# Matmuls of tiles 0, 2 and 4 extended over 16, 32 and 56 columns of the next tile in a fused convolution kernel

## The reference

```python
def _L0_conv_ref(x, dw_weight, pw_weight, pw_bias):
    h = conv_general_dilated(x, dw_weight, padding=((1, 1), (1, 1)), feature_group_count=C)   # 3x3 depthwise
    h = gelu(h)
    maps = einsum('bchw,oc->bohw', h, pw_weight) + pw_bias[None, :, None, None]
    maps = maps.reshape(B, 8, C, H, W)
    out = zeros_like(x)
    for i, (dx, dy) in enumerate(OFFSETS8):
        diff = roll(x, shift=(dy, dx), axis=(-2, -1)) - x
        out = out + maps[:, i] * diff
    return out

x = x + _L0_conv_ref(_gn(x), dw_weight, pw_weight, pw_bias)
```

## Time and profile before

| | |
|---|---|
| runs shown | 2279.0 and 2280.24 us, median 2279.62 us |
| span of the profiled execution, first to last instruction | 2255.6 us |
| median less span | 24.0 us |
| TensorE matmul busy | 2201.9 us, 98% of the span, 10752 matmuls |
| VectorE busy | 2067.1 us, 92% |
| mean granted TensorE clock | 1.000 |

### The profile page before, as it was taken

How to read it: one execution, slowest core, us unless ns; L and a number is a source line. 1 busy time by engine, 2 the same in 40 slices (tenths; PEclk the granted TensorE clock), 3 DMA queues, 4 the chain that set the end, 5 groups by cost and what they waited for, 6 DMA issues and landing times.

```text
span 2255.6 us, 28700 instructions
## 1 busy us (share of the span) xinstructions
PE 2201.9 (98%) x10752; PEld 2014.8 (89%) x10752; DVE 2067.1 (92%) x2234; ACT 1842.6 (82%) x2762; POOL 1976.3 (88%) x857
## 2 busy tenths in 40 slices
PE   1999999999999999999999999999999999999998
PEld 1999999999999999999999999999999999999997
DVE  7999999999999999989999899999999999989895
ACT  5979888798888978888788887878878788787774
POOL 5889998999989988898888988889889998988985
PEclk9999999999999999999999999999999999999999
DMA  6245372543626444263443725337254372543424
GB/s 180 49 84 118 50 143 62 107 97 56 150 33 123 98 84 105 50 129 76 90 99 51 145 58 102 88 64 157 33 106 96 53 155 34 106 99 50 98 33 74
DMA packets 47083, 202.13 MB, mean 90 GB/s; under 512 B 3040, under 2 KB 7136, under 8 KB 45664
## 3 DMA queue, kind: packets, MB, share of 16 engines
q0 software_dynamic: 30192, 94.97, 26.1%
q1 hardware_dynamic: 16752, 105.34, 18.2%
HBM read 104.88 MB, written 146.80 MB: 112 GB/s over the span
## 4 chain that ended last, share of the span: by engine, by line
PE 92%; DVE 5%; ACT 1%; issue 1%; DMA 0%; POOL 0%; SPq 0%; DVEq 0%; ACTq 0%
PE psum L914 92%; DVE psum L775 2%; DVE products L702 1%; DVE psum L784 1%; DVE psum L702 0%; DMA acc<-x 0%; ACT psum L587 0%; ACT psum L555 0%; DVE acc L724 0%; ACT hid L569 0%; DVE acc L756 0%; POOL hlo L332 0%; DVE fields L807 0%; DVE part_sums L794 0%; DVE products L759 0%
## 5 line engine op out<-in xcount | busy, mean ns | idle before, releaser
L587 ACT ACTIVATE psum<-psum,bias,rstd 128x448 f32<-128x448 f32 x1792 | 1203.9, 694 | 368.6 <-PE psum L914 364.1
L914 PE MATMUL psum<-hhi,w_hi 128*128 128x448 f32 x3584 | 1312.7, 366 | 46.1 <-ACT hhi L574 45.4
L363 POOL TENSOR_TENSOR acc<-acc,products 128x896 f32<-128x896 f32 x333 | 1162.7, 3491 | 205.5 <-DVE products L702 197.6
L914 PE MATMUL psum<-hhi,w_lo 128*128 128x448 f32 x3584 | 1311.7, 366 | 0.0
L914 PE MATMUL psum<-hlo,w_hi 128*128 128x448 f32 x3584 | 1022.3, 366 | 0.3 <-POOL hlo L332 0.3
L784 DVE SCALAR_TENSOR_TENSOR psum<-xn,dw_f,psum 128x896 f32<-128x896 f32 x768 | 881.5, 1148 | 72.4 <-ACT psum L559 66.7
L914 PEld LDWEIGHTS psum<-hhi,w_hi 128*128 128x128 f32 x3584 | 671.9, 187 | 109.7 <-issue 45.4
L914 PEld LDWEIGHTS psum<-hlo,w_hi 128*128 128x128 f32 x3584 | 671.5, 187 | 62.2 <-POOL hlo L332 0.9
L914 PEld LDWEIGHTS psum<-hhi,w_lo 128*128 128x128 f32 x3584 | 672.0, 187 | 61.3
L702 DVE TENSOR_TENSOR products<-psum,fields 128x896 f32<-128x896 f32 x555 | 600.9, 1083 | 24.1 <-ACT psum L587 22.8
L702 DVE TENSOR_TENSOR acc<-psum,fields 128x896 f32<-128x896 f32 x224 | 241.6, 1086 | 45.8 <-ACT psum L587 45.3
(11 more groups left out here) (67 smaller groups left out, 448.2 us busy)
## 6 DMA issues: line engine op xcount, KB each, us to landing
out<-acc POOLq DMA_DIRECT2D x96, 896.0 KB, 7.7
out<-x SPq DMA_DIRECT2D x16, 3136.0 KB, 12.8
xpad<-x SPq DMA_DIRECT2D x30, 1568.0 KB, 14.8
out<-acc POOLq DMA_DIRECT2D x15, 448.0 KB, 5.6
acc<-x SPq DMA_DIRECT2D x4, 784.0 KB, 6.8
xpad<-pw_t SPq DMA_DIRECT2D x1, 2048.0 KB, 12.2
out<-products SPq DMA_DIRECT2D x2, 224.0 KB, 1.9
dw_f<-dw SPq DMA_DIRECT2D x1, 9.0 KB, 8.1
```

What stands on the lines that cost most here:

```text
L363: nc.gpsimd.tensor_tensor(a, a, p, ALU.add).then_inc(added_s, 1)
L587: nc.scalar.activation(m, m, ACT.Identity, bias=bias[ip][:, g, d:d + 1], scale=rstd[ip][:, g:g + 1]).then_inc(biased_s, 1)
L914: last = nc.tensor.matmul(maps(n0 * UNITS + q)[:, side, :], w[:, kk, col:col + P], h_part(h, t, nl, kk), start=s == 0, stop=s == len(steps ...
```

## The change

`make_maps` gets a width for each tile: 448 columns, and for tiles 0, 2 and 4 of every image 464, 480 and 504. The moving operand then runs on over the first 16, 32 or 56 columns of the odd tile behind it in the slot, and the output into columns 448 and up of the same bank, which nothing reads. Number and order of the instructions, weights, waits and signals stay.

```diff
+        def maps_wide(q, width):
+
+            b = 2 * (q % MAP_GROUPS)
+            return psum[:, b:b + 2, 0:width]
+
...
+        def h_wide(h, t, nl, kk, width):
+
+            if width == PX:
+                return h_part(h, t, nl, kk)
+            return h[:, H_SLOT[nl - t + 2 * (t // 2) + kk]].rearrange("p t x -> p (t x)")[:, 0:width]
...
         @block.tensor
         def _(pe):
+            SPILL = {0: 16, 2: 32, 4: W}
+
             def make_maps(n0, nl, u):
 
                 t, q = nl % TILES, nl * UNITS + u
 
+                width = PX + SPILL.get(t, 0)
...
-                        last = nc.tensor.matmul(maps(n0 * UNITS + q)[:, side, :], w[:, kk, col:col + P], h_part(h, t, nl, kk),
+                        last = nc.tensor.matmul(maps_wide(n0 * UNITS + q, width)[:, side, :], w[:, kk, col:col + P],
+                                                h_wide(h, t, nl, kk, width),
                                                 start=s == 0, stop=s == len(steps) - 1)
```

## The result

The changed kernel takes 2332.3 us (2330.95 and 2333.62), the kernel before 2279.6: slower by 52.7 us, where 27.9 were forecast. The quotient of these medians is 1.023; the ratio of the runs near the fastest of each kernel is 1.0247, 95% interval 1.021 to 1.0285. The profiled execution of the changed kernel took 2330.95 us with a span of 2329.2, so 1.8 us lie around the span, and not 24.0. The kernel before turns out to scatter by 3% from one execution to the next (2213 to 2280 us over 71 timed runs, these two among them), so the experiments are told by median and range, and the size of the slowdown depends on which of its executions one compares with: it is 2.3% against the two here, and 5% against the quickest. The 1.8 us already say that the profiled execution of before (span 2255.6) and its two timed runs (2279.6) weren't equally long.

The account below looks back on a forecast made before the run. The prediction took TensorE's stream of 10752 matmul steps to bound the kernel. Added columns +66.6, slow steps -46.6, redrawn pace +10.2 and stalls -2.3 gave +27.9 us on 2279.6, that is 2307.5 us, range 2250 to 2370.

Parts of the forecast that it names:

- The 24.0 us around the span: Whole run: 24.0 us of the 2279.6 us were taken to lie outside the profiled span of 2255.6 us.
- two-pace reading: TensorE's matmul stream in the profile: the same matmul steps at 200.0 or 206.7 ns, about 6980 of 10752 at the latter.
- The 46.6 us of slow steps: TensorE: 6980 matmuls at 206.7 ns cost 6.7 ns each over 200.0 ns; 46.6 us was subtracted.
- The pace is drawn anew some 96 times: Borders of tiles 0, 2 and 4: six step-length changes per image each redraw the pace, some 96 times instead of 7.
- one slow step in seven: All 10752 matmuls after the change: a seventh at 206.7 instead of 200.0 ns, adding 10.2 us; ends 0 and 71.7.
- rival A: From the border of tiles 0 and 1, first image, every matmul pays 20.0 ns over its stream: 2369 us; chance 0.30.
- The upper value: Wide tiles 0, 2, 4: each added column costs 0.4167 ns, steps of 206.7, 213.3 and 223.3 ns, 66.6 us in all.
- rival B: Wide tiles: columns nearly free, steps of 200.0 ns up to 480 columns and 210.0 at 504; 2255 us; chance 0.24.
- the 0.11 us between two weight loads: Stalled place at 130.74 us: next load starts at 130.85, so loads aren't what a step waits for and columns cost.
- The sign that the prediction named for a failure on columns: Wide tiles' steps not 6.7, 13.3 and 23.3 ns over their neighbours' would mean the column cost is wrong.
- The six waits: Unit 2 of tile 4: six stalls waiting for VectorE, 2.3 us in all, vanish because tile 4's first 24 matmuls take longer.
- Rival C: Whole stream: a disturbance brings steps to their bare stream length, 186.7 ns at 448 columns; 2152 us; chance 0.06.

Follow-up runs that it names:

- only0: Kernel before with tile 0 alone of each image widened, by 16 columns; 2284.2 us.
- after_again: The changed kernel run again without an edit; 2331.8 us median of 4 runs (2331.4 to 2334.8).
- narrow: Kernel before with tile 1 of image b cut to 448 - 8 b columns (448 to 328), leaving out columns of the result; 2199.4 us.
- ladder: Kernel before with tiles 0, 2 and 4 of image b at 448 + 4 b columns (448 to 508); 2307.1 us.
- mend: The changed kernel with the last unit (12 matmuls) of tile 0 at 500 columns instead of 464; 2297.3 us (2296.3 to 2298.1, 4 runs).

## Why the prediction was wrong

**The time around the span: wrong, 22 of the 24.0 us.** "The 24.0 us around the span" failed. Every later run has 1.7 to 1.9 us there. The profiled execution of before was quick for a third of its length; its two timed runs, at 2279.0 and 2280.2 us, lie where a stream slow from the start does (2255.6 + 25.1 - 2.3 + 1.8 = 2280.2). The text used the two-pace reading within the trace and didn't ask whether another execution would share it. The 46.6 us of slow steps, taken as something the change would give back, was 71.7 us in the runs that were the yardstick, and is 0 in others.

**The pace: wrong, and the step that mattered most.** "The pace is drawn anew some 96 times" failed, and with it the one slow step in seven. A change of width is no draw. Single wide matmuls left the quick pace in 24 of 32 cases, near the six of seven assumed, but in all 29 cases that can be compared the second execution did as the first. A wide tile of 96 equal matmuls settles into a repeating pattern, and what it hands on follows from its width and what it found: slow after slow at all 44 wide tiles behind the one that threw the changed kernel's profiled run, quick after quick behind 480 and 504 in its image 0. Of the change's widths only 464 turned quick to slow, at both tiles (one here, one in only0) that found the quick pace and ended at that width. Since no width of the change leads back and the stalls are gone, slow is the end of every run. What does vary from run to run is the start and the stalls, which the prediction counted with the borders as one kind of disturbance. The mechanism is rival A's, with its place right (the border of tile 0) and its image off by one, or not at all in after_again, which is slow from tile 1 of image 0 on. Its price of 2369 us was high by the misread 24.0 us (22 of it) and by the column costs below.

**The columns: right in kind, short in size on the quick pace, long on the slow one.** "The upper value", stream plus 13.3 ns, was named as a bound from above; over the quick step 464, 480 and 504 columns cost 12.2, 16.7 to 17.8 and 26.7 ns instead of 6.7, 13.3 and 23.3; over the slow step 5.5, 10.0 and 20.0. That they cost at all, against rival B, was argued from the 0.11 us between two weight loads, and narrow and ladder bear it out. The sign that the prediction named for a failure on columns came: the wide tiles' steps aren't 6.7, 13.3 and 23.3 ns over their neighbours'. The slope that the Trainium skill gives (TensorE: Matmul & The Clock Gate, "Back-to-back issue gap") is borne out on the mean: from 328 to 508 columns the step grows by 77.7 ns, where 180 / 2.4 is 75.0. Its 2.5 ns of fixed cost, which that section gives for an isolated matmul and not for a stream of weight loads and matmuls, fits no row here, the least being 12.3.

**The stalls: right for the profiled execution.** The six waits are gone, with the cover of tile 4's first 24 matmuls. A slow stream has no stall, so the timed runs of before, if slow throughout, had no 2.3 us to give back.

**The sum with what was measured.** From the profiled execution of before: columns over the quick step 1536 x (12.2 + 16.7 + 26.7) ns = +85.4; 60 slow tiles x 96 x 6.67 ns = +38.4, in place of the 46.6 before; stalls -2.3: +74.9, against 73.6 us between the spans. From the timed runs, slow throughout: 1536 x (5.5 + 10.0 + 20.0) ns = 54.5, less image 0's four quick tiles, 2.6: +51.9, against 52.7. Term by term against the forecast: columns 54.5 for 66.6, slow steps -2.6 for -46.6 + 10.2 = -36.4, stalls 0 for -2.3. The slow steps are thus 33.8 us off, more than the whole miss of 24.8, and the columns hid a part of it. That the two timed runs of before were slow throughout is inferred from their times; no trace of one is kept. Rival C's third pace was never seen at 448 columns.

## What to carry to other kernels

Where one engine's step repeats ten thousand times, read the distance of its starts along the whole span before anything else: two stable values are possible at one granted clock, and a single profile then doesn't stand for the timed runs. Check that the profiled execution's span plus a small constant gives the timed run; a gap of 1% is another execution, not overhead. Columns that cost little a piece can cost much by what they leave behind (34 us between the changed kernel and mend), and a short stretch of the right width can fix the pace; which width that is has to be measured. Before calling an outcome chance, compare two traces of one kernel place by place: here what looked like a draw came out alike in 44 of 44 places.

## What the runs showed of the hardware that wasn't expected

At a granted clock of 1.00 a stream of weight load and 448-column matmul runs at 200.0 or at 206.7 ns a step and keeps either for thousands of steps. From 452 to 508 columns the mean steps are mostly multiples of 3.33 ns, 15 to 19 ns over the stream, and not in order: 468 columns (210.0 ns) are faster than 464 (212.2), and 492 to 500 cost the same 223.3. Tiles of 480 and 504 columns hold the two paces apart inside themselves, as two patterns of steps, and tiles of 464 don't. What makes the grid, and why 500 columns lead to the quick pace from both sides while 464 lead away from it, no run here shows; what sets the pace at the start of a run is open as well.
